# Relational graph network on 100,000 nodes: layer 1 multiplies 112 of 196 blocks, the output stage multiplies 42 parts itself, and implied waits are dropped

## The chip, the cores and the metric

The kernel runs on one core of a Trainium2 chip. The core has TensorE (PE, with weight loads shown as PEld), VectorE (DVE), ScalarE (ACT), GpSimd (POOL) and SyncE (SP), and 16 DMA engines, which the queues of SP (q1), ACT (q10) and POOL (q0, indirect transfers whose descriptors POOL makes itself) share. The metric is the device time of one execution in microseconds. The median of three runs before the change is 3426.85 us (3426.82 to 3428.76); the profiled execution took 3434.24 us, of which the span from first to last instruction is 3432.4 us.

## The reference

```python
h = jnp.maximum(_layernorm(x, axis=-1), 0.0)
x = x + _L0_gnn_ref(h, weight, w_comp, h_bias, src, dst, edge_type_16)
h = jnp.maximum(_layernorm(x, axis=-1), 0.0)
x = x + _L1_gnn_ref(h, enc_w, enc_b, lin_l_w, lin_l_b, lin_r_w, edge_index)   # edge_index = [src, dst]
# _L0: message of an edge = h[src] @ (sum_b w_comp[type, b] * weight[b]); summed by dst; + h_bias
# _L1: h = leaky(x @ enc_w + enc_b)
#      for l in 0, 1:
#          agg = segment_sum(h[src], dst) / max(degree, 1)
#          h = leaky(agg @ lin_l_w[l] + lin_l_b[l] + h @ lin_r_w[l])     (leaky slope 0.1)
```

x is 100,000 x 128 float32 and there are 50,000 edges, sorted by dst. The destinations are drawn as 100000 * u^2, so low rows have most edges.

## The kernel before

The edges are padded to 392 tiles of 128 (56 "half steps" of 7 tiles). Four stages run one after the other, each with its own buffers and semaphores; after a short preparation they are, in the order of the code:

- **Relational stage** (`relational_pass`, 56 steps of 7 tiles). POOL gathers x rows of an edge tile (L368) six steps ahead; DVE takes the norm's statistics (L793 to L808), ACT normalizes (L894), PE transposes and multiplies with the eight bases (L973), ACT and DVE mix the eight products (L912, L826), PE sums runs of equal dst with a 0/1 matrix (`same`, L984), DVE carries a run over the tile's edge (L838), ACT adds the bias (L920) and keeps the rows in one of two buffers of 7 tiles (`rows`, L927), and POOL scatters them to `agg` (L704). In POOL's order one gather of step m and one scatter of step m-6 alternate, and ACT's `keep_rows` of tile (m, j) waits for the scatter of tile (m-2, j) to land. SP meanwhile fills `agg` with the bias (four transfers of 1 MB in each of the first steps, each waiting for the one before the last), stores gathered x rows, and zeroes `means1` and the right half of `pair`. Rows that a scatter must not keep go to spare rows behind row N.
- **Node stage** (`node_pass`): x1 = x + agg, norm, encoder, and layer 0's two products; `pair` holds for each node 128 numbers of h @ lin_r and 128 of the mean's product. POOL again alternates gathers (L1102) and scatters (L1111).
- **Layer 1** (`layer_pass`, the names end in `_l`). POOL gathers 1 KB rows of `pair` for every edge tile (L1722, a ring of three half steps: the gather of step m waits for DVE's addition of step m-3, `s_mixed`). DVE adds the two halves and applies leaky (L1830, L1833); PE sums runs and multiplies with lin_l (L1930, L1938); ACT scales the rows to means (L1885) and stores them by edge, keeping the last eight half steps on chip. In between, a sweep over all nodes makes z1 = leaky(pair sum) @ lin_r + bias: 196 blocks of 512 nodes, seven in each two half steps: SP loads 512 KB of `pair` (L1541), DVE adds and applies leaky (L1550, L1553), PE transposes and multiplies (L1564, L1578, L1582), ACT copies (L1572, L1590) and stores 256 KB to z1 (L1597).
- **Output stage.** POOL puts the means by dst into `means1` (L1727), last half step first; for all but the eight kept ones SP first loads 448 KB back (L1791), and that load waits for the puts of two steps ago. At the same time ACT's queue walks 98 parts of 1024 nodes from the last node down: it loads x1 and z1 three parts ahead (L1684, L1685), waits until enough half steps are put (`wait_final`) and loads the means (L1689), and stores the result of two parts ago (L1696); DVE adds z and mean, applies leaky and adds x1 (L1655, L1658, L1661). Everything on ACT stands in one written order:

```python
for k in range(COUNT + STORED_AFTER):      # STORED_AFTER, LOADED_BEFORE = 2, 3
    if k < COUNT:
        load_means(k)
    if k >= STORED_AFTER:
        store(k - STORED_AFTER)
    if k + LOADED_BEFORE < COUNT:
        load(k + LOADED_BEFORE)
```

## Time and profile before

| | us |
|---|---|
| median of 3 runs | 3426.85 |
| profiled execution | 3434.24 |
| its span | 3432.4 |
| PE / DVE / ACT / POOL busy | 2372.6 / 2910.6 / 1909.4 / 2497.7 |

A share of busy time is an average over the four stages. POOL's instructions here are descriptor generation, each followed by about 0.3 us that the profile calls "issue" and does not count as busy, so POOL can be without a gap and still show 70 to 80%. "DMA" is the busy share of the 16 DMA engines. A row of the timeline gives start, duration, engine, line and names, and in brackets how long the engine stood idle before it and what released it.

### The profile page before, as it was taken

What the parts mean: (1) busy time and instruction counts of PE and PEld (TensorE: products, weight loads), DVE (VectorE), ACT (ScalarE), POOL (GpSimd) and SP (SyncE); (2) the same over time, 40 slices, a digit from 0 to 9 for tenths busy, and PEclk for the clock granted to TensorE, in tenths of its full rate; (3) what the DMA queues carried; (4) which work ended last, traced back from release to release, by engine and by line L of the source; (5) the groups of instructions that cost most, each with busy time, mean ns of one, the idle gap of its engine ahead of it and who ended that gap; (6) DMA issues with size and microseconds to landing.
All of it is one profiled execution on the core that took longest, in us unless ns stands there. A gap on an engine that the chain in (4) does not pass through costs nothing. (4 is left out here: it accounts for less than half of the span.)

```text
span 3432.4 us, 57476 instructions
## 1 busy us (share of the span) xinstructions
PE 2372.6 (69%) x13942; PEld 1758.7 (51%) x13942; DVE 2910.6 (85%) x8326; ACT 1909.4 (56%) x4979; POOL 2497.7 (73%) x2364
## 2 busy tenths in 40 slices
PE   2999999999998688888888888488888860000000
PEld 2555555555554466666666666388778760000000
DVE  4999999899897799999999999699999966555665
ACT  1666666566665688888888888255555540000000
POOL 4777777777776677777777776677777747677675
PEclk9999999999999899999999999799999985555555
DMA  9988888886222899999999997599999979999998
GB/s 242 387 294 263 260 256 257 252 244 178 84 76 66 295 287 282 285 283 282 288 280 289 281 288 219 179 393 401 397 395 395 398 281 412 414 414 414 408 412 313
DMA packets 663813, 1016.37 MB, mean 296 GB/s; under 512 B 73669, under 2 KB 406343, under 8 KB 657058
## 3 DMA queue, kind: packets, MB, share of 16 engines
q1 hardware_dynamic: 487190, 555.28, 49.8%
q10 hardware_dynamic: 94758, 285.20, 21.5%
q0 software_dynamic: 81536, 172.20, 15.1%
q8 instruction: 121, 1.98, 0.2%
q14 instruction: 208, 1.70, 0.1%
HBM read 534.94 MB, written 485.83 MB: 297 GB/s over the span
## 5 line engine op out<-in xcount | busy, mean ns | idle before, releaser
L973 PE MATMUL y_ps_rel<-w_basis,ht_rel 128*128 128x512 f32 x1568 | 745.0, 598 | 0.1
L1722 POOL DMA_INDIRECT gat_l<-base_and_means,src_c x392 | 469.7, 1198 | 123.9 <-issue 118.8
L704 POOL DMA_INDIRECT agg<-rows_rel,put_c x392 | 410.8, 1048 | 135.5 <-issue 98.7
L1270 ACT ACTIVATE h_node<-base_node,shift_node,rstd_node 128x128 f32<-128x128 f32 x1176 | 500.5, 483 | 1.6 <-DVE shift_node L1360 1.6
L368 POOL DMA_INDIRECT gat_rel<-in_x_dram,src_c x392 | 403.7, 1030 | 125.0 <-issue 106.5
L1111 POOL DMA_INDIRECT base_and_means<-rows_node,odd_c x392 | 388.9, 992 | 145.3 <-issue 118.0
L1102 POOL DMA_INDIRECT term_node<-agg,src_c x392 | 395.1, 1008 | 132.9 <-issue 119.7
L1727 POOL DMA_INDIRECT means<-late_l,put_c x336 | 366.9, 1092 | 160.7 <-issue 94.2
L826 DVE SCALAR_TENSOR_TENSOR two_rel<-y_ps_rel,coef,two_rel 128x128 f32<-128x128 f32 x1568 | 437.5, 341 | 3.2 <-DVE two_rel L826 1.8
L973 PEld LDWEIGHTS y_ps_rel<-w_basis,ht_rel 128*128 128x128 f32 x1568 | 269.6, 192 | 192.0 <-issue 131.1
L1655 DVE TENSOR_TENSOR last_z_l<-last_z_l,node_done_l 128x1024 f32<-128x1024 f32 x98 | 120.2, 1226 | 255.9 <-DMA node_done_l<-means 255.8
L984 PEld LDWEIGHTS sum_ps_rel<-same_rel,two_rel 128*128 128x128 f32 x1568 | 237.3, 192 | 188.6 <-issue 111.2
L912 ACT ACTIVATE part_rel<-y_ps_rel,coef 128x128 f32<-128x128 f32 x784 | 243.1, 362 | 139.8 <-PE y_ps_rel L973 139.0
L826 DVE SCALAR_TENSOR_TENSOR two_rel<-y_ps_rel,coef,part_rel 128x128 f32<-128x128 f32 x784 | 237.0, 343 | 77.6 <-ACT part_rel L912 77.3
L1184 PE MATMUL ht_ps_node<-ident,h_node 128*128 128x128 f32 x1176 | 188.8, 283 | 119.6 <-ACT h_node L1270 119.5
L1330 DVE BATCH_NORM_STATS2 st_node<-base_node 128x6 f32<-128x128 f32 x1176 | 256.5, 281 | 10.2
L1184 PEld LDWEIGHTS ht_ps_node<-ident,h_node 128*128 128x128 f32 x1176 | 129.0, 142 | 221.5 <-ACT h_node L1270 221.1
L984 PE MATMUL sum_ps_rel<-same_rel,two_rel 128*128 128x128 f32 x1568 | 238.7, 275 | 0.6 <-DVE sums_rel L838 0.6
L927 ACT ACTIVATE rows_rel<-row_ps_rel 128x128 f32<-128x128 f32 x392 | 108.9, 278 | 203.9 <-PE row_ps_rel L992 130.1
L1582 PEld LDWEIGHTS z_ps_l<-w_r,ht_l 128*128 128x128 f32 x1568 | 209.7, 194 | 7.9
L1217 PEld LDWEIGHTS z_ps_node<-w_r,g_t_node 128*128 128x128 f32 x1568 | 208.2, 193 | 6.6
L1572 ACT ACTIVATE ht_l<-ht_ps_l 128x512 f32<-128x512 f32 x196 | 117.2, 598 | 168.1 <-PE ht_ps_l L1564 124.1
(183 smaller groups left out, 5988.8 us busy)
## 6 DMA issues: line engine op xcount, KB each, us to landing
pairs_l<-base_and_means SPq DMA_DIRECT2D x196, 512.0 KB
base_and_means<-zero_row SPq DMA_DIRECT2D x49, 1024.0 KB
means<-zero_row SPq DMA_DIRECT2D x49, 1024.0 KB
first_node<-in_x_dram SPq DMA_DIRECT2D x196, 256.0 KB
term_node<-agg SPq DMA_DIRECT2D x196, 256.0 KB
x<-base_node SPq DMA_DIRECT2D x196, 256.0 KB
base_and_means<-done_node SPq DMA_DIRECT2D x196, 256.0 KB
z<-node_done_l ACTq DMA_DIRECT2D x196, 256.0 KB
```

What stands on the lines that cost most here:

```text
L368: nc.gpsimd.indirect_dma_start(gat_rel[:, m % X_RING, j, :], None, x, bass.IndirectOffsetOnAxis(ap=src_c[:, m * HALF + j:m * HALF + j + 1] ...
L704: nc.gpsimd.indirect_dma_start(agg, bass.IndirectOffsetOnAxis(ap=put_c[:, t:t + 1], axis=0), rows[:, q, j, :], None).then_inc(s_scattered[ ...
L826: nc.vector.scalar_tensor_tensor(acc[:, a, :], y[:, b * P:(b + 1) * P], c, prior, ALU.mult, ALU.add).then_inc(s_acc, 1)
L973: nc.tensor.matmul(y_ps[(q + j) % 2][:, c * 512:(c + 1) * 512], ht[:, q, j, :], w_basis[:, 4 * c:4 * c + 4, :], start=True, stop=True).the ...
L984: last = nc.tensor.matmul(sum_ps[s][:, 0:P], two[:, j, a, :], same[:, q, j, :], start=(a == 0), stop=(a == 1))
L1102: nc.gpsimd.indirect_dma_start(term[:, q, j * P:(j + 1) * P], None, agg, bass.IndirectOffsetOnAxis(ap=src_c[:, t:t + 1], axis=0)).then_inc ...
L1111: nc.gpsimd.indirect_dma_start(pair.rearrange("n (k f) -> (n k) f", k=2), bass.IndirectOffsetOnAxis(ap=odd_c[:, t:t + 1], axis=0), rows[:, ...
L1184: last = nc.tensor.transpose(ht_ps[n % 2][:, j * P:(j + 1) * P], h[:, n % 2, j * P:(j + 1) * P], ident[:])
L1270: last = nc.scalar.activation(h[:, n % 2, j * P:(j + 1) * P], base[:, n % SLOTS, j * P:(j + 1) * P], ACT.Relu, bias=shift[:, b % 2, c:c + ...
L1330: nc.vector.bn_stats(st6[:, n // 3 % 2, n % 3, j, :], base[:, n % SLOTS, j * P:(j + 1) * P]).then_inc(s_stat, 1)
L1722: nc.gpsimd.indirect_dma_start(gat[:, g, j, :], None, source, bass.IndirectOffsetOnAxis(ap=src_c[:, t:t + 1], axis=0)).then_inc(s_gathered ...
L1727: nc.gpsimd.indirect_dma_start(means1, bass.IndirectOffsetOnAxis(ap=put_c[:, t:t + 1], axis=0), rows_, None, bounds_check=N - 1, oob_is_er ...
```

## The change

Seven things are changed.

1. Layer 1's sweep (`SWEEP = 4` instead of 7) makes four blocks in two half steps, 112 in all. The first 98 are stored to z1 as before. The last 14 (`stays`) are the two halves of each of the last seven parts of nodes; ACT copies their products into the slots of `last_z`, where the output stage finds them, and they aren't stored.
2. The output stage takes the first 7 parts from these slots. For the next 42 parts (`again`) it loads 1 MB of `pair` instead of 512 KB of z1 (`load_pair`), DVE adds and applies leaky (`mix`), PE transposes (`turn_again`), ACT copies (`keep_turned_again`), PE multiplies (`product_again`), and DVE adds the mean to the product in PSUM. The last 49 parts are as before, with z1.
3. In the relational stage the ring of `rows` has three half steps (`KEPT = 3`), with one semaphore for each; ACT waits at j = 0 for all seven scatters of step m-3.
4. The spare rows are doubled (3584), and all of them in `agg` and in both halves of `pair` are zeroed by two transfers at SP's step 2; POOL's first scatter waits for both. Before, 1792 rows of the left half of `pair` were zeroed at the end of the stage.
5. The seven BATCH_NORM_AGGREGATE of a half step and the addition of EPS become five small operations.
6. Waits that another wait implies are left out on DVE, ACT and PE in all stages. POOL's waits stay.
7. In `message` the wait for the low half of the products stands one operation earlier.

```diff
-        SPARE = 2 * HALF * P
+        SPARE = 4 * HALF * P
...
+            KEPT = 3
...
-                rows = buf("rows", [P, 2, HALF, P])
+                rows = buf("rows", [P, KEPT, HALF, P])
...
                         def scatter(m, j):
-                            q, t = m % 2, m * HALF + j
+                            t = m * HALF + j
                             if j == 0:
                                 wait_bias(pool, m)
+                            if m == 0 and j == 0:
+                                pool.wait_ge(s_spare, 2 * DMA)
                             pool.wait_ge(s_rows, tile(m, j))
...
                             spill(m)
+                            if m == 2:
+                                sp.dma_start(agg[N:N + SPARE, :].rearrange("(p j) f -> p j f", p=P),
+                                             zero_row[:].unsqueeze(1).to_broadcast([P, SPARE // P, P])).then_inc(s_spare, DMA)
+                                sp.dma_start(pair[N:N + SPARE, :].rearrange("(p j) (k f) -> p (j k) f", p=P, f=P),
+                                             zero_row[:].unsqueeze(1).to_broadcast([P, SPARE // P * 2, P])).then_inc(s_spare, DMA)
...
-                            for j in range(HALF):
-                                wait_apart(dve, s_dve_passed, (s_stat, tile(m, j)))
-                                nc.vector.bn_aggr(mv[:, q, j, :], st6[:, q, j, :]).then_inc(s_mv, 1)
-                            dve.wait_ge(s_mv, tile(m, HALF - 1))
-                            nc.vector.tensor_scalar(var[:, q, :], mv[:, q, :, 1], EPS, None, ALU.add).then_inc(s_var, 1)
+                            dve.wait_ge(s_stat, tile(m, HALF - 1))
+                            nc.vector.tensor_tensor(apart[:], half[:, :, 1], half[:, :, 4], ALU.subtract).then_inc(s_small, 1)
...
                         def keep_rows(m, q, j):
                             act.wait_ge(s_rowed, tile(m, j))
-                            if at_least(m, 2):
-                                act.wait_ge(s_scattered[q][j], use(m - 2, q))
+                            if m >= KEPT and j == 0:
+                                act.wait_ge(s_scattered[m % KEPT], HALF * DMA * (m // KEPT))
...
-                    return [[(0, 0), (2, 1), (4, 2), (6, 3)], [(1, 4), (3, 5), (5, 6)]][r]
+                    return [[(0, 0), (4, 1)], [(1, 2), (4, 3)]][r]
+                def stays(w, i, c):
+                    return i * w.walk + c >= STORED
...
+                    if stays(w, i, c):
+                        k, a = part_and_half(w, i, c)
+                        result = last_z[:, k, a * BLOCK:(a + 1) * BLOCK]
...
+                AGAIN = COUNT - SLOTS_OUT - STORED // 2
+                def again(k):
+                    return SLOTS_OUT <= k < SLOTS_OUT + AGAIN
...
+                    def mix(k):
+                        dve.wait_ge(s_out[c], k // WALK * DMA)
+                        dve.wait_ge(s_pair[d], (n // len(last_pair) + 1) * DMA)
+                        nc.vector.tensor_tensor(node_.rearrange("p (j f) -> p j f", f=P), last_pair[d][:, :, 0:P],
+                                                last_pair[d][:, :, P:2 * P], ALU.add).then_inc(s_remixed, 1)
...
+                        if again(k):
+                            dve.wait_ge(s_rez, n + 1)
+                            for a in range(2):
+                                nc.vector.tensor_tensor(last_z[:, c, a * BLOCK:(a + 1) * BLOCK], rez_ps[n % 2][a][:],
+                                                        last_m[c][:, a * BLOCK:(a + 1) * BLOCK], ALU.add).then_inc(s_both, 1)
...
+                    for k in range(COUNT):
+                        if again(k + 1):
+                            mix(k + 1)
+                        combine(k)
+                def turn_again(pe, n):
+                    pe.wait_ge(s_releaked, n + 1)
...
+                def product_again(pe, n):
+                    pe.wait_ge(s_reht, n + 1)
...
                         if k >= STORED_AFTER:
                             store(k - STORED_AFTER)
-                        if k + LOADED_BEFORE < COUNT:
+                        if again(k):
+                            keep_turned_again(act, k - SLOTS_OUT)
+                        if again(k + LOADED_BEFORE):
+                            load_pair(k + LOADED_BEFORE)
+                        if SLOTS_OUT <= k + LOADED_BEFORE < COUNT:
                             load(k + LOADED_BEFORE)
```

SP in the relational stage, step 2 (line numbers are those of the changed kernel; L749 loads a step's run starts, L729 stores gathered x rows, L164 fills `agg`, L753 and L755 zero the spare rows):

```order
+L749 DMA run_b_rel<-run_in_tile 128x896 [waits open_made_rel,same_made_rel]
+L729 DMA x_by_edge<-gat_rel 128x896 [waits gathered2_rel]
+L753 DMA agg<-zero_row 3584x1x128
+L755 DMA base_and_means<-zero_row 7168x1x128
+L164 DMA agg<-fill_rows 128x2048 [waits agg_filled1]
```

The two zeroing transfers stand in front of step 2's four fills; before, the first fill followed the x rows directly.

DVE in layer 1, one half step in the middle, before the change:

```order
L1830 TENSOR_TENSOR act_gat_l<-gat_l 128x896
L1833 SCALAR_TENSOR_TENSOR act_gat_l<-act_gat_l 128x896
L1550 TENSOR_TENSOR node_done_l<-pairs_l 128x512
L1553 SCALAR_TENSOR_TENSOR node_done_l<-node_done_l 128x512
L1845 SCALAR_TENSOR_TENSOR sums_l<-open_l,sums_l,sum_ps_l 128x128 x2
L1550 TENSOR_TENSOR node_done_l<-pairs_l 128x512
L1553 SCALAR_TENSOR_TENSOR node_done_l<-node_done_l 128x512
L1845 SCALAR_TENSOR_TENSOR sums_l<-open_l,sums_l,sum_ps_l 128x128 x2
L1814 TENSOR_TENSOR same_l<-run_b_l,run_c 128x896
L1550 TENSOR_TENSOR node_done_l<-pairs_l 128x512
L1553 SCALAR_TENSOR_TENSOR node_done_l<-node_done_l 128x512
```

and the same place in the changed kernel:

```order
L1886 TENSOR_TENSOR act_gat_l<-gat_l 128x896
L1889 SCALAR_TENSOR_TENSOR act_gat_l<-act_gat_l 128x896
L1899 SCALAR_TENSOR_TENSOR sums_l<-open_l,sums_l,sum_ps_l 128x128 x2
L1523 TENSOR_TENSOR node_done_l<-pairs_l 128x512
L1526 SCALAR_TENSOR_TENSOR node_done_l<-node_done_l 128x512
L1899 SCALAR_TENSOR_TENSOR sums_l<-open_l,sums_l,sum_ps_l 128x128 x2
L1874 TENSOR_TENSOR same_l<-run_b_l,run_c 128x896
L1899 SCALAR_TENSOR_TENSOR sums_l<-open_l,sums_l,sum_ps_l 128x128
L1881 TENSOR_SCALAR open_l<-run_b_l 128x896
L1523 TENSOR_TENSOR node_done_l<-pairs_l 128x512
L1526 SCALAR_TENSOR_TENSOR node_done_l<-node_done_l 128x512
```

Of the node sweep's pairs of operations three or four stand in a half step before, two now; the rest of DVE's order is as it was.

ACT in the output stage, one part before the change:

```order
L1689 DMA node_done_l<-means 128x1024
L1696 DMA out_dram<-last_z_l 128x1024
L1684 DMA pairs_l<-x 128x1024
L1685 DMA last_z_l<-z 128x1024
L1668 TENSOR_LOAD need_l
```

and one of the 42 parts in the changed kernel:

```order
L1746 DMA same_l<-means 128x1024
L1753 DMA out_dram<-last_z_l 128x1024
L1712 ACTIVATE ht_l<-ht_ps_l 128x512 x2
L1741 DMA pair_more_l<-base_and_means 128x2048
L1732 DMA pairs_l<-x 128x1024
L1717 TENSOR_LOAD need_l
```

Two ACTIVATEs, which wait for PE's transposes of this part, now stand between the store and the next loads, and a transfer of `pair` of twice the size stands in the place of z1's.

## Rows read from the trace of the kernel before

**Rows 1.** Stages: us, busy (x) of PE, PEld, DVE, ACT, POOL, clock, DMA share, GB/s
```profile
77.00:1122.00 1045.00, 960.00 (x3920) 562.42 (x3920) 936.69 (x3817) 659.70 (x2129) 784.43 (x758) 0.98 0.70 218
1122.00:2181.00 1059.00, 868.35 (x5782) 687.19 (x5782) 993.94 (x3137) 912.79 (x2058) 784.17 (x786) 0.98 0.90 274
2181.00:2774.00 593.00, 490.75 (x3865) 458.57 (x3866) 557.13 (x960) 310.08 (x734) 469.61 (x392) 0.96 1.01 384
...
2836.00:3406.00 570.00, 0.00 (x0) 0.00 (x0) 343.15 (x280) 0.00 (x0) 402.10 (x368) 0.50 1.03 412
```

**Rows 2.** Waits in the relational stage, 230 to 1100 us: total, times, longest
```profile
ACT rows_rel L927 <- DMA agg<-rows_rel,put_c: 73.1, 65, 3.0
...
POOL agg L704 <- ACT rows_rel L927: 25.2, 54, 2.6
```

**Rows 3.** Timeline of POOL: the first scatter
```profile
103.39 1.00 POOL L704 DMA_INDIRECT agg<-rows_rel,put_c  x1 [5.65 <-ACT rows_rel L927]
```

**Rows 4.** DVE's comparison of the run starts, once a step, 130 to 240 us
```profile
L778 DVE TENSOR_TENSOR same_rel<-run_b_rel,run_c x6: 1081/1082/1084, 134.7 to 222.9; 128x896 f32<-128x896 uint8 x6
```

**Rows 5.** Timeline of SP's queue before and in step 2
```profile
79.44 11.19 SPq L164 DMA_DIRECT2D agg<-fill_rows  x4
...
91.17 0.53 SPq L725 DMA_DIRECT2D x_by_edge<-gat_rel  x1
```

**Rows 6.** DMA queue of SP, 400 to 1000 us: packets, MB, share of 16 engines
```profile
q1 hardware_dynamic: 150416, 90.51, 51.9%
```

**Rows 7.** Layer 1: the page's gathers; their durations; DVE's sweep by line, 2240 to 2770
```profile
L1722 POOL DMA_INDIRECT gat_l<-base_and_means,src_c x392 | 469.7, 1198 | 123.9 <-issue 118.8
...
L1722 POOL DMA_INDIRECT gat_l<-base_and_means,src_c x392: 945/1115/9587, 2181.0 to 2773.1; - x196
...
L1553 DVE SCALAR_TENSOR_TENSOR node_done_l<-node_done_l 128x512 f32<-128x512 f32 x173 | 119.7, 692 | 6.0
...
L1550 DVE TENSOR_TENSOR node_done_l<-pairs_l 128x512 f32<-128x512 f32 x173 | 118.2, 683 | 0.1
```

**Rows 8.** Timeline of one long gather and DVE's operation beside it
```profile
2336.79 1.08 DVE L1814 TENSOR_TENSOR same_l<-run_b_l,run_c 128x896 f32<-128x896 uint8 x1
...
2337.01 1.77 POOL L1722 DMA_INDIRECT gat_l<-base_and_means,src_c  x1 [0.30 <-issue]
```

**Rows 9.** Timeline, POOL and DVE: early in layer 1, then its end
```profile
2259.06 1.33 POOL L1722 DMA_INDIRECT gat_l<-base_and_means,src_c  x1 [0.30 <-issue]
...
2267.92 1.08 DVE L1830 TENSOR_TENSOR act_gat_l<-gat_l 128x896 f32<-128x896 f32 x1
...
2773.07 0.94 POOL L1722 DMA_INDIRECT gat_l<-base_and_means,src_c  x1 [0.30 <-issue]
2814.41 1.02 POOL L1727 DMA_INDIRECT means<-kept_rows_l,put_c  x1 [40.39 <-ACT kept_rows_l L1885]
...
2793.00 1.08 DVE L1830 TENSOR_TENSOR act_gat_l<-gat_l 128x896 f32<-128x896 f32 x1
```

**Rows 10.** DMA from 2814 to 3432 us: GB/s in 40 slices, totals, ACT's queue
```profile
GB/s 300 390 416 415 416 416 414 414 416 413 415 415 414 414 414 416 414 414 414 415 415 413 413 414 413 413 413 390 409 406 413 413 413 412 410 406 404 410 169 137
DMA packets 75632, 244.72 MB, mean 396 GB/s; under 512 B 13440, under 2 KB 14281, under 8 KB 75616
...
q10 hardware_dynamic: 56448, 205.55, 82.5%
```

**Rows 11.** Timeline of PE: four transposes twice, then eight matmuls
```profile
2207.19 1.06 PE L1564 MATMUL ht_ps_l<-ident,node_done_l 128*128 128x128 f32 x4
...
2212.54 0.60 PE L1564 MATMUL ht_ps_l<-ident,node_done_l 128*128 128x128 f32 x4
...
2213.20 1.05 PE L1582 MATMUL z_ps_l<-w_r,ht_l 128*128 128x128 f32 x8
```

**Rows 12.** The page's rows of ACT's copy and DVE's addition
```profile
L1655 DVE TENSOR_TENSOR last_z_l<-last_z_l,node_done_l 128x1024 f32<-128x1024 f32 x98 | 120.2, 1226 | 255.9 <-DMA node_done_l<-means 255.8
...
L1572 ACT ACTIVATE ht_l<-ht_ps_l 128x512 f32<-128x512 f32 x196 | 117.2, 598 | 168.1 <-PE ht_ps_l L1564 124.1
```

More of the change, by code:

```diff
@@ L712, in _ @@
                                     scatter(m - lag, j)
-                        for q in range(2):
-                            for j in range(HALF):
-                                pool.wait_ge(s_scattered[q][j], DMA * HALVES // 2)
+                        for k in range(KEPT):
+                            pool.wait_ge(s_scattered[k], HALF * DMA * len(range(k, HALVES, KEPT)))
                     @block.sync
@@ L1670, in wait_base @@
                 def wait_base(act):
-                    act.wait_ge(s_need, 1)
-                    for c in range(sweep.walk):
-                        act.wait_ge(sweep.s_stored[c], DMA * walks)
+                    for c in range(SWEEP):
+                        act.wait_ge(sweep.s_stored[c], DMA * len(range(c, STORED, SWEEP)))
                 def write_out(act):
@@ L1698, in write_out @@
                     wait_base(act)
-                    for k in range(LOADED_BEFORE):
+                    act.wait_ge(s_need, 1)
+                    for k in range(SLOTS_OUT):
                         load(k)
@@ L1956, in _ @@
                             ago(HALVES, 0, 0, j, 3, to_rows)
+                        for n in range(AGAIN):
+                            turn_again(pe, n)
+                            product_again(pe, n)
             clear(held)
```

256 lines of the change are left out of this document (129 added, 127 removed).

## Prediction

> **What bounds the kernel now.** I read the stages first [rows 1]. In the output stage the 16 DMA engines are full (share 1.03, 412 GB/s) and PE and ACT are empty; in layer 1 they are full too (1.01, 384 GB/s), but something else is also full there. So I read POOL. Its share of busy time looks harmless, because about 0.30 us after each transfer aren't counted [rows 8, 9]. With them a gather of layer 1 takes 1.198 us + 0.30 [rows 7], and 392 of them fill 588 of the stage's 593 us; only 5.0 us go to waits for DVE. In the relational stage POOL's mean is 784.43 / 758 = 1.035 us [rows 1], and a step has 7 gathers and 7 scatters: 14 x 1.335 = 18.7 us. DVE, left alone, makes a step in (222.9 - 134.7) / 5 = 17.64 us [rows 4]. POOL falls behind by a microsecond a step until ACT finds no free buffer: 65 stalls, 73.1 us [rows 2]. The reader should see that this isn't time to be won: in 870 us POOL waited 25.2 us for rows [rows 2]. POOL sets the pace of this stage. The node stage is alike: 784.17 us in 786 transfers, with 0.30 each 1020 of 1059 us [rows 1], and nothing is changed on POOL there.
>
> **The change, part by part**, against the profiled execution's 3434.24 us.
>
> *Relational stage, third buffer and dropped waits: 0.* They free ACT and DVE, which POOL already outruns. The wait at j = 0 for all of step m-3 lets POOL be later by about one tile's time at the stage's end, 1 us. The five small operations of DVE take the place of eight; DVE has a microsecond a step to spare, so they count nothing. If POOL weren't the pace, DVE's 17.64 us would come true instead of 18.7: 50 steps x 1.06 = -53 us; that is the lower bound of this item, the upper is +5 (small operations with two SBUF inputs in POOL's way).
>
> *Zeroing of the spare rows: +14 us.* Two transfers of 3584 and 7168 rows of 512 B go in front of step 2's fills, and the first scatter, which stood at 103.39 us [rows 3], now waits for them. Behind it in POOL's order stand all later gathers and scatters. SP reaches the place at 91.17 + 0.53 us [rows 5]; the four fills before it took 11.19 us, 2.8 each, and two of them are under way, with the 448 KB spill behind: start about 98 us. Price: a packet of this queue, while it mostly writes 512 B zeros, took 0.519 x 16 x 600 us / 150,416 = 33 ns of one engine [rows 6]; 10,752 packets over 16 engines are 22 us. They land at about 120 us, 16.6 after 103.39, of which POOL gets back the wait of 1 to 2 us that followed. Since POOL never idles afterwards, it goes through to the end: +14. Bounds: 0 (if the engines take the zeros first) and +20. The .9 MB zeroing that leaves the end of the stage was hidden there: 0.
>
> *Node stage: 0*, -5 to +5.
>
> *Layer 1, the gathers: -22 us.* The shortest gather is 945 ns, the mean 1198 [rows 7]. What is the rest? The gather at 2337.01 began 0.22 us into DVE's comparison of 1.08 us and took 1.77 us, that is, the comparison's remaining 0.86 us (less a little) longer [rows 8]. So a gather that meets a long DVE operation with two SBUF inputs waits for its end. Random arrivals meet an operation of length t in proportion to t and lose t/2: the sum of t²/2 over a half step is 3.5 x (0.683² + 0.692²)/2 = 1.65 for the sweep [rows 7], and 3 x 1.08²/2 = 1.75 for the comparison and the two additions over the gathered rows [rows 8]. The sweep's 1.65 becomes 2 x 0.473 = 0.95: together 3.40 to 2.70, x 0.79. In a step shortened from 10.6 to 10.2 us they come denser: the excess of 0.253 us becomes 0.21. A half step is then 7 x (0.945 + 0.21 + 0.30) = 10.2 us, and 56 of them 571 instead of 593. Bounds: no excess left, 56 x 8.7 = 488 (-105); the excess unchanged, 0. DVE, at 557 of 593 us [rows 1], loses 84 x 1.4 = 118 us of work; DMA falls from 228 MB (593 us x 384) to 158: neither is near. That is where most of the expected gain stays out: the sweep was cut by 43%, but POOL gathers as before.
>
> [...]
>
> *Layer 1, its end: -17 us.* The last gather starts at 2773.07, DVE adds its half step at 2793.00, and the first put is at 2814.41 [rows 9]. Early in the stage that first distance was 2267.92 - 2260.4 = 7.5 us instead of 19: DVE had fallen behind to the depth of the ring. With 118 us less work it doesn't: -12. The last 21.4 us hold DVE's and ACT's last blocks and stores; half of the blocks and all stores of the end go: -5. Bounds -5 and -27.
>
> *Output stage: +34 us.* Before, 244.72 MB [rows 10] at 412 GB/s [rows 1] are 594 us; the stage has 618 (2814.4 to 3432.4), the other 24 being the start (300 and 390 GB/s in the first slices of 15.45 us: 5 us) and the end (169 and 137: 19 us [rows 10]), where the last part waits for the last put. Now 49 parts load no z1 (49 x 0.524 = -25.69 MB; 98 before) and 42 load 1.049 MB of `pair` (+44.04): 263.07 MB, 638.5 us. The start stays 5. The puts, 604 us long before, end ahead of the transfers, so the end is only the last part's additions and store, 8 us: 651.5, +33.5. The added work must hide: DVE per part 2 x 1.23 for `mix` and about 4.0 to combine [rows 12], 6.5 us; one part is 2.62 MB at 412 less the 69 GB/s of the puts and loads back ((244.72 - 205.55) MB / 570 us [rows 10]), 7.6 us. It hides, with 1 us of room. Bounds: +25 (start gap gone too) and +55 (below).
>
> Sum: 14 - 22 - 17 + 34 = +9. Profiled 3443 us; as this execution was 7.4 above the median, the median is forecast at 3426.85 + 9 = **3436 us**.
>
> **Rivals.**
>
> *Slow clock in the output stage (slower).* The chain of one part is PE transposes, ACT's two copies (1.15 us [rows 12]), PE products, and PE takes the next part's transposes only after that. At the upper clock it is short: 8 transposes 1.05, 16 products and two bias products 2.4 [rows 11], with two hand-overs of 0.25: 5.1 us. At the lower level (1.2 GHz, as at 2207.19, where four transposes took 1.06 instead of 0.60 us [rows 11]) it is 1.9 + 1.15 + 4.6 + 0.5 = 8.15 us a part. It decides from 7.6 us on: 42 x 0.55 = +23, so 3459. For it: PE stands still 40 us before and has half a part's time idle in each part. Against it: between 2207.19 and 2212.54 the same kind of work brought the upper level back [rows 11]. No row shows work with pauses like these.
>
> *The relational stage gains (faster).* If ACT's 73.1 us of stalls, not POOL, cost the time, a third buffer gives up to -53; I take half, -26 instead of 0: 3410. Against it stand POOL's waits of 25.2 us in 870.
>
> *Gathers near their floor (faster).* If DVE's and POOL's steps lock so that they seldom meet, half of the excess goes: 56 x 9.6 = 538, -55 instead of -22: 3403. The steps here are regular, so phase matters; nothing says which.
>
> *The zeroing is hidden (same).* If it lands before about 105 us: +9 - 14 = -5, 3422.
>
> *The change doesn't do what it says:* product and store of fewer blocks, but no time; that is nearly the forecast's own statement, since -39 and +34 cancel.
>
> **How the numbers follow.** Forecast 45%, slow clock 17%, relational gain 9%, gathers near the floor 9%, zeroing hidden 12%, others 8%. A measurement of this kernel can tell 0.2%, 7 us, from no change: slower is above 3434, faster below 3420. The forecast's own range, from the bounds, is 3418 to 3455; of its 45%, 27 are slower, 15 the same and 3 faster. Slower: 27 + 16 (slow clock) + 3 (hidden) + 4 (others) = 50%. Same: 15 + 1 + 7 (hidden) + 3 = 26%. Faster: 3 + 8 + 8 (the two faster rivals) + 2 + 3 = 24%. The range that leaves out 2 in 10 goes from 3403 to 3463.
>
> **What would show it.** Right: the first scatter near 120 us, POOL without waits after it and the first node gather (1122 before) near 1136; gathers of layer 1 with a mean of 1.15 us and the first put 41 - 17 = 24 us after the last gather; the output stage at 412 GB/s from the first parts to the end, 263 MB, the last put some 45 us before the last store. Wrong: a relational step below 18 us in the middle; a gather mean below 1.08; an output stage in which the DMA share falls below 1 in the 42 parts (the slow clock, or the written order on ACT).

## The result, and the profile after

The changed kernel takes 3400.98 us (median of 4 runs, 3400.85 to 3402.68), the kernel before on the same chip 3427.81 us (4 runs): a ratio of 0.9921, with a 95% interval of 0.9904 to 0.9939. It is 27 us faster. Ratios leave out executions that took over 1.5% longer than the fastest of the same kernel. The forecast was 3436 us, 9 us slower, with a range from 3403: both the sign and the range were wrong.

The profiled execution has a span of 3399.1 us (3432.4 before). Its stages, in the columns of [rows 1]; the fourth line is the output stage, the fifth the 42 parts that are made again:

```profile
77.00:1147.00 1070.00, 969.20 (x3920) 568.78 (x3920) 930.39 (x3649) 664.73 (x2129) 786.38 (x757) 0.97 0.70 217
1147.00:2203.00 1056.00, 865.72 (x5782) 685.23 (x5782) 992.26 (x3137) 911.91 (x2058) 782.41 (x786) 0.98 0.90 275
2203.00:2716.00 513.00, 380.46 (x2870) 352.43 (x2871) 464.29 (x812) 243.85 (x582) 393.60 (x392) 0.95 0.94 320
2741.00:3399.00 658.00, 204.05 (x1092) 176.63 (x1092) 463.46 (x420) 45.58 (x84) 421.80 (x392) 0.62 1.00 400
2783.00:3106.00 323.00, 204.05 (x1092) 176.63 (x1092) 261.19 (x255) 45.58 (x84) 219.58 (x201) 0.75 1.02 414
```

The reader should see two things. Layer 1's gathers take 513 us instead of 593 with POOL's 392 transfers at 393.60 us instead of 469.61 [rows 1]; the forecast had 571. And in the parts made again the DMA engines are full (1.02) though PE's clock is at 0.75 in the mean.

| stretch | before | after | difference | forecast |
|---|---|---|---|---|
| up to the first gather of layer 1 | 2181.0 | 2202.9 | +21.9 | +14 |
| gathers of layer 1 | 592.1 | 511.9 | -80.2 | -22 |
| last gather to first put | 41.3 | 26.8 | -14.5 | -17 |
| output stage | 618.0 | 657.4 | +39.4 | +34 |
| sum | | | -33 | +9 |

(us of the profiled executions; the medians of the runs differ by 27.)

**Start.** The timelines of POOL and of SP's queue (start, duration, idle time before it and what ended it), which answer to [rows 3, 5]:

```profile
128.01 0.99 POOL L709 DMA_INDIRECT agg<-rows_rel,put_c  x1 [31.05 <-DMA base_and_means<-zero_row]
...
92.24 11.20 SPq L164 DMA_DIRECT2D agg<-fill_rows  x4
103.55 0.39 SPq L749 DMA_DIRECT2D run_b_rel<-run_in_tile  x1
104.39 0.54 SPq L729 DMA_DIRECT2D x_by_edge<-gat_rel  x1
104.98 1.06 SPq L753 DMA_DIRECT2D agg<-zero_row  x1
106.09 7.51 SPq L755 DMA_DIRECT2D base_and_means<-zero_row  x1
```

The first scatter stands at 128.01, not near 120. SP reaches step 2 only at 103.55: the row at 91.17 of [rows 5], which I took for step 2's, was step 1's, and another four fills of 11.20 us lie between. The price was right: issued at 104.98, released at 128.01 are 23 us, against the 22 that I worked out.

**Relational stage.** The waits from 230 to 1100 us, which answer to [rows 2]:

```profile
ACT rows_rel L925 <- DMA agg<-rows_rel,put_c: 39.0, 23, 2.1
POOL agg L709 <- ACT rows_rel L925: 17.1, 56, 0.3
```

ACT's stalls fell from 73.1 to 39.0 us, and the stage took as long as before: first to last scatter 1005.2 us (128.0 to 1133.2), before 1004.4.

**Layer 1.** The page's row of the gathers and the spread of their durations, which answer to [rows 7]; below them POOL and then DVE in the middle of the stage:

```profile
L1784 POOL DMA_INDIRECT gat_l<-base_and_means,src_c x392 | 393.7, 1004 | 119.7 <-issue 119.7
...
L1784 POOL DMA_INDIRECT gat_l<-base_and_means,src_c x392: 942/946/10308, 2202.9 to 2714.8; - x196
...
2500.28 0.94 POOL L1784 DMA_INDIRECT gat_l<-base_and_means,src_c  x1 [0.30 <-issue]
2501.53 0.94 POOL L1784 DMA_INDIRECT gat_l<-base_and_means,src_c  x1 [0.30 <-issue]
...
2499.26 1.08 DVE L1886 TENSOR_TENSOR act_gat_l<-gat_l 128x896 f32<-128x896 f32 x1
2500.38 1.09 DVE L1889 SCALAR_TENSOR_TENSOR act_gat_l<-act_gat_l 128x896 f32<-128x896 f32 x1
```

The median gather is now at the floor of 0.94 us. Look at the place of DVE's two long operations, both with two SBUF inputs: the first ends at 2500.34, 0.06 us after a gather's start, the second starts at 2500.38, 0.10 us after it. One gather starts every 0.94 + 0.30 = 1.24 us, two of DVE's operations of 1.08 us are 1.12 apart, and neither costs POOL anything.

**End of layer 1.** POOL's last gather and first put, which answer to [rows 9]:

```profile
2714.85 0.95 POOL L1784 DMA_INDIRECT gat_l<-base_and_means,src_c  x1 [0.30 <-issue]
2741.67 1.02 POOL L1789 DMA_INDIRECT means<-kept_rows_l,put_c  x1 [25.88 <-ACT kept_rows_l L1939]
```

**Output stage.** DMA from 2742 to 3399 us: GB/s in 40 slices of 16.4 us, and the totals, which answer to [rows 10]:

```profile
GB/s 313 289 410 418 416 417 416 416 418 417 416 415 416 415 417 417 417 414 415 417 415 398 400 414 413 414 414 413 412 413 413 413 404 413 412 403 389 407 405 168
DMA packets 74614, 263.14 MB, mean 401 GB/s; under 512 B 13328, under 2 KB 14169, under 8 KB 69209
```

263.14 MB were moved, where 263.07 were worked out.

### The profile page after: what moved, and what is told of

The parts are those of the page before. It is cut to its first block and busy times, and to the rows that moved or that the text cites. A ratio compares the mean times of both kernels' runs of the same rounds, so it can differ in the third digit from the quotient of the medians.

```text
span 3399.1 us, 49875 instructions
## 1 busy us (share of the span) xinstructions
PE 2460.3 (72%) x13942; PEld 1821.4 (54%) x13942; DVE 2901.5 (85%) x8116; ACT 1885.1 (55%) x4895; POOL 2417.1 (71%) x2364
## 3 DMA queue, kind: packets, MB, share of 16 engines
q14 instruction: 165, 1.35, 0.1%
## 5 line engine op out<-in xcount | busy, mean ns | idle before, releaser
L972 PE MATMUL y_ps_rel<-w_basis,ht_rel 128*128 128x512 f32 x1568 | 754.9, 605 | 3.7 <-DVE two_rel L831 3.7
L1784 POOL DMA_INDIRECT gat_l<-base_and_means,src_c x392 | 393.7, 1004 | 119.7 <-issue 119.7
L1984 PE MATMUL sum_ps_l<-same_l,act_gat_l 128*128 128x128 f32 x784 | 169.5, 299 | 153.9 <-DVE sums_l L1899 112.8
L1712 ACT ACTIVATE ht_l<-ht_ps_l 128x512 f32<-128x512 f32 x84 | 45.6, 595 | 312.9 <-PE ht_ps_l L1692 312.9
L1984 PEld LDWEIGHTS sum_ps_l<-same_l,act_gat_l 128*128 128x128 f32 x784 | 119.8, 193 | 176.0 <-DVE act_gat_l L1889 149.8
```

The source lines that it names most:

```text
L972: nc.tensor.matmul(y_ps[(q + j) % 2][:, c * 512:(c + 1) * 512], ht[:, q, j, :], w_basis[:, 4 * c:4 * c + 4, :], start=True, stop=True).the ...
L1784: nc.gpsimd.indirect_dma_start(gat[:, g, j, :], None, source, bass.IndirectOffsetOnAxis(ap=src_c[:, t:t + 1], axis=0)).then_inc(s_gathered ...
L1984: nc.tensor.matmul(sum_ps[(q + j) % 2][:, 0:P], act_gat[:, q, j, :], same[:, q, j, :], start=True, stop=True).then_inc(s_summed, 1)
```

## The experiments

Theory after the result: a gather of layer 1 lasts 0.945 us, and longer only where it starts inside a DVE operation that holds it up; the excess (what a gather takes over 0.945 us) fell further than I had thought. Rivals: the 16 DMA engines, full before (1.01), lengthened the gathers; the third buffer won time. Medians are compared with the kernel before on the same chip (ratio, 95% interval). A trace is of one execution, and not always of a typical one; where it took much longer or shorter than the median, the text says so.

**The zeroing, and the relational stage.** In the first kernel the spare rows of `agg` are zeroed ahead of step 0's fills, and those of `pair` at the stage's end; the first scatter waits for the former alone:

```diff
-                            if m == 2:
+                            if m == 0:
                                 sp.dma_start(agg[N:N + SPARE, :] ...
-                                sp.dma_start(pair[N:N + SPARE, :] ...
...
+                        sp.dma_start(pair[N:N + SPARE, :] ...
```

> The changed kernel, with the spare rows of agg zeroed ahead of the fills of step 0 (not of step 2), the first scatter waiting for those alone, and the spare rows of base_and_means zeroed at the end of the relational stage. Theory (the late first scatter goes through to the end, since POOL sets the pace of the stage): first scatter back at 103 to 106 us (128.0 in the changed kernel, 103.4 before), last one at 1108 to 1111, and the whole 22 to 25 us faster than the changed kernel: 3376 to 3379. Rival (POOL catches up in the stage, so that the delay cost little): last scatter near 1125 to 1133, gain below 8 us.

Measured: 3388.52 us, ratio 0.9885 (0.987 to 0.990): 12.5 us less than the changed kernel, half of what I expected. First scatter at 103.1, last at 1116.2. But the profiled execution took 3401.71 us, 13 above the median and as long as the changed kernel, so its rows don't show what a typical one won.

The second is the changed kernel with the whole old `relational_pass` and 3584 spare rows.

> The changed kernel with the relational stage of the kernel before (two row buffers, all of its waits, bn_aggr, 3584 spare rows and their zeroing at the end); layer 1 and the output stage as changed. Theory (the third buffer and the dropped waits are worth nothing, POOL sets the pace; only the zeroing cost): first gather of the node stage at 1122, as before, and 22 to 26 us faster than the changed kernel: 3375 to 3379, the same as with the zeroing moved. Rival (the third buffer gains, hidden by the zeroing): slower than the kernel with the zeroing moved by what the buffer is worth, by the 73 - 39 us of ACT's stalls up to 34 us.

Measured: 3375.61 us (5 runs), ratio 0.9847 (0.9834 to 0.986), 25 us below the changed kernel, as expected (profiled: 3384.96). It is **faster than both kernels**. First scatter at 104.3, last at 1108.9. From first to last scatter it takes 1004.6 us, the changed kernel 1005.2: the third buffer and the dropped waits gained nothing. With the zeroing hidden the new stage took 1013.1 in the one execution that was profiled, the long one; the medians point the same way, since that kernel is 12.9 us slower than the one with the old stage. POOL's transfers sum to 820 us there and to 811 in the old stage, and POOL waits 45.7 us for rows instead of 36.6. Where the transfers met DVE's comparison, the excess over 945 ns was 33 against 27 us; to the five small operations I put about 2. That is most of the 9 us of transfers, not a cause that was shown. The run meant for it changed only the mean and variance back:

> The kernel with the zeroing moved, with the mean and variance of the kernel before (bn_aggr on one SBUF input, seven times a step) in place of the five small operations on DVE, four of them with two SBUF inputs. With the zeroing moved the relational stage ended at 1116.2 us, with the old stage at 1108.9, and its gathers and scatters took 820 us against 811. Theory (the small operations hold POOL up, as those of layer 1 do): last scatter at 1107 to 1111 us, POOL's transfers 811 to 815 us, the whole 5 to 10 us faster than with the zeroing moved alone. Rival (the third buffer or the dropped waits or the place of the zeroing cost it): last scatter 1114 to 1118, no change of the whole.

It fell on a chip on which both kernels took longer (4162.27 us, the kernel before 4177.82; ratio 0.994, 0.9896 to 0.9985), and can't be set beside the others. Why the new stage costs time stays open.

**More and fewer blocks.** `SWEEP` 5 and 3, other lists of places (with 3, `store` also skips a block that does not exist, and one more buffer holds means):

```diff
-                SWEEP = 4
+                SWEEP = 5          # the other kernel: 3
-                    return [[(0, 0), (4, 1)], [(1, 2), (4, 3)]][r]
+                    return [[(0, 0), (2, 1), (4, 2)], [(1, 3), (4, 4)]][r]   # 3: [[(0, 0), (4, 1)], [(2, 2)]]
```

> The changed kernel with 5 blocks of the sweep per two half steps (places (0, 2, 4) and (1, 4)) instead of 4: 126 blocks stored, 28 parts made again. Theory (gathers are lengthened by DVE's operations with two SBUF inputs, which meet them more often again): gather mean 1.04 to 1.10 us, layer 1's gathers 530 to 550 us (513 with 4, 593 with 7), output stage 13 us shorter than 657, whole 3408 to 3425. Rival (the gathers' time goes by what the 16 DMA engines have to move): the bytes of layer 1 rise from 164 to about 186 MB, 362 GB/s in 513 us, below the 384 to 416 that the engines did: gathers stay at 513 to 518 us, whole 3388 to 3395.

> The changed kernel with 3 blocks per two half steps (places (0, 4) and (2)): 70 blocks stored, 56 parts made again. Theory: the excess over 945 ns, already 59 ns in the mean, shrinks only a little (gather mean 0.97 to 0.99, gathers 500 to 508 us), the output stage grows by 14 x 0.94 = 13 us, the end of layer 1 is some 3 us shorter: 3394 to 3405, no gain. Rival (excess in proportion to the sweep, 80 us for three blocks): 27 us off the gathers, 3382 to 3390.

Measured: with 5 blocks 3404.72 us (0.9934, 0.9919 to 0.9949), gather mean 1.043, gathers 527 us, as the theory had it, the gathers and the whole each 3 us under its range. With 3 blocks 3453.41 us (1.0078, 1.0063 to 1.0094): **less work on DVE, less on the DMA, and the gathers take 551 us instead of 512**, mean 1.104. With 3 blocks the theory and its rival both missed. How much DVE does was not the point.

**The same work at other places.**

```diff
-                    return [[(0, 0), (4, 1)], [(1, 2), (4, 3)]][r]
+                    return [[(1, 0), (5, 1)], [(2, 2), (6, 3)]][r]
```

> Again the changed kernel with the four blocks at the places (1, 5) and (2, 6), on a chip that runs at the usual speed. After the runs so far the theory is another: whether an operation of DVE stands where a gather starts is a matter of where the operations are, not of how little DVE does (with 3 blocks the mean was 1.104, with 4 at (0, 4), (1, 4) it was 1.004). Expected: gather mean 1.08 to 1.17 us as on the slow chip (1.157), gathers of layer 1 545 to 575 us, whole 30 to 60 us slower than the changed kernel. Rival (DVE that keeps up is enough, the slow chip spoilt the first try): mean 0.98 to 1.05, gathers 505 to 530 us.

Measured: 3475.64 us, ratio 1.0145 (1.012 to 1.0169), 75 us above the changed kernel, where I expected 30 to 60. Here is the same stretch of that kernel: the page's row, POOL, DVE.

```profile
L1784 POOL DMA_INDIRECT gat_l<-base_and_means,src_c x392 | 468.3, 1195 | 119.7 <-issue 119.7
...
2500.38 1.35 POOL L1784 DMA_INDIRECT gat_l<-base_and_means,src_c  x1 [0.30 <-issue]
2502.03 1.43 POOL L1784 DMA_INDIRECT gat_l<-base_and_means,src_c  x1 [0.30 <-issue]
...
2499.82 1.09 DVE L1886 TENSOR_TENSOR act_gat_l<-gat_l 128x896 f32<-128x896 f32 x1 [2.90 <-DMA gat_l<-base_and_means,src_c]
2501.96 0.68 DVE L1523 TENSOR_TENSOR node_done_l<-pairs_l 128x512 f32<-128x512 f32 x1
```

Every operation is the one of the changed kernel; the mean is back at 1.195 us (1.198 before) and the gathers at 586 us. The first gather starts with 0.53 us of the addition left and takes 1.35 us, 0.40 over 0.945; the second with 0.61 us left, 0.48 over. So what is left of the operation, less 0.13 us, is added. The whole gain of layer 1 hangs on four numbers in a list.

**DVE's load and the DMA's load, one at a time.** One kernel gives DVE 84 pairs of operations more in layer 1 (on a scratch buffer, at places of their own), the other SP 112 loads of 512 KB more that nobody reads:

```diff
+  nc.vector.tensor_tensor(pair_more[:, 4:6, :] ..., pair_more[:, 0:4, 0:P], pair_more[:, 0:4, P:2 * P], ALU.add)
+  nc.vector.scalar_tensor_tensor(pair_more[:, 4:6, :], pair_more[:, 4:6, :], SLOPE, pair_more[:, 4:6, :], ALU.mult, ALU.max)
```

```diff
+  for a in range(2):
+      sp.dma_start(pair_more[:, 4 * a:4 * a + 4, :], pair[m * BLOCK:m * BLOCK + BLOCK, :] ...)
```

> Again the changed kernel with DVE's old work in layer 1 (84 further pairs of operations on a scratch buffer), on a chip at the usual speed. Theory (gathers are lengthened by DVE's operations with two SBUF inputs and by nothing else): gather mean 1.15 to 1.22 us, gathers 570 to 600 us with the DMA engines at 280 to 290 GB/s. Rival (the DMA load made them long): mean 0.99 to 1.03.

> Again the changed kernel with 58.7 MB of further loads in layer 1, on a chip at the usual speed. Theory: gathers that start in no two-input operation of DVE take 0.945 us as ever; 223 MB at 412 GB/s are 541 us, so that layer 1's gathers take 535 to 560 us, the addition of waiting for data (over 20 us) and not of longer gathers; mean 0.97 to 1.08 (the places shift). Rival (full DMA engines lengthen the gather itself): also gathers that meet no operation of DVE are longer than 1.0 us.

Measured: 3492.29 us (1.0193, 1.0169 to 1.0218) and 3467.91 us (1.0122, 1.0097 to 1.0147). Their layer 1, in the columns of [rows 1]:

```profile
2204.00:2793.00 589.00, 419.20 (x2834) 388.78 (x2834) 560.34 (x961) 239.38 (x577) 458.27 (x392) 0.88 0.86 277
...
2204.00:2776.00 572.00, 391.98 (x2834) 362.64 (x2834) 463.38 (x802) 242.04 (x577) 434.31 (x392) 0.93 1.01 384
```

With DVE's old work and 277 GB/s the gathers take as long as before (mean 1.170): less traffic alone does not make them short. With full engines they take 572 us, longer than the 541 that the bytes need and longer than I expected, and the mean is 1.108. But in that kernel DVE waits 65.2 us for `run_b` loads, which now queue behind the further ones, and so stands at other places. Of 349 gathers, 153 meet a long operation and carry 51.4 of the 51.8 us of excess; the other 196 took 0.947 us in the mean, with the engines full. The DMA doesn't lengthen a gather; it moves DVE.

**The rule over all kernels.** For each gather (the first 29 and last 14 left out, 349 stay) I took what was left, at its start, of a DVE operation with two SBUF inputs; where this was over 0.15 us, it less 0.13 us is what the rule adds:

| kernel | gathers us | mean us | that meet one | excess over 0.945, sum us | by the rule | DVE waits for rows | POOL waits for DVE |
|---|---|---|---|---|---|---|---|
| before | 592 | 1.198 | 236 | 82.2 | 77.0 | 1.4 | 5.0 |
| changed | 512 | 1.004 | 78 | 11.8 | 8.8 | 2.9 | 0 |
| old relational stage | 512 | 1.004 | 73 | 12.2 | 8.6 | 0 | 0.3 |
| 5 blocks | 527 | 1.043 | 102 | 25.1 | 22.0 | 3.1 | 0 |
| 3 blocks | 551 | 1.104 | 131 | 48.0 | 49.4 | 42.8 | 0 |
| other places | 586 | 1.195 | 178 | 80.8 | 80.1 | 53.4 | 0 |
| DVE more | 588 | 1.170 | 207 | 72.1 | 64.8 | 0 | 17.0 |
| DMA more | 571 | 1.108 | 153 | 51.8 | 49.4 | 3.4 | 28.9 |
| zeroing moved | 518 | 1.017 | 86 | 16.5 | 12.7 | 0.8 | 2.2 |
| before, other places | 589 | 1.188 | 203 | 79.2 | 73.4 | 0.6 | 6.6 |
| pieces, marks on ACT | 521 | 1.028 | 105 | 20.4 | 39.6 | 11.4 | 0 |
| pieces | 548 | 1.050 | 89 | 29.0 | 25.7 | 0 | 22.1 |

(The last three kernels are described below.) The rule gives the excess of every kernel but one to within 8 us, from 9 to 80. For "pieces, marks on ACT" it gives twice the measured excess. Two gathers of that kernel, each with DVE's operation beside it, show why:

```profile
2309.40 0.95 POOL L1784 DMA_INDIRECT gat_l<-base_and_means,src_c  x1 [0.30 <-issue]
2309.36 0.77 DVE L1526 SCALAR_TENSOR_TENSOR node_done_l<-node_done_l 128x512 f32<-128x512 f32 x1
...
2344.93 1.46 POOL L1784 DMA_INDIRECT gat_l<-base_and_means,src_c  x1 [0.30 <-issue]
2344.88 0.69 DVE L1526 SCALAR_TENSOR_TENSOR node_done_l<-node_done_l 128x512 f32<-128x512 f32 x1
```

The first operation began 0.04 us before the gather: the gather lost nothing, and the operation took 0.77 us itself. The second began 0.05 us before, took its usual 0.69 us, and the gather lost 0.52. In this kernel 26 gathers began less than 0.045 us behind such an operation; the rule adds 20.2 us for them, and they carry 0.01. Without them it gives 19.4 for 20.4 us. In the 20 traces together 61 gathers that began up to 0.043 us behind an operation were free, and of 104 held ones that began up to 0.12 us behind it all but one stood at 0.045 or more. So the remainder counts only where the operation came first by some 0.045 us. I read this off the traces; no run was made to test it.

The last two columns (from the views of the waits) show what goes with few meetings: in four quick kernels (changed, old relational stage, zeroing moved, 5 blocks) DVE hardly waits for gathered rows, nor POOL for DVE's addition. Where DVE does wait for rows, the landing of a transfer starts its additions, at any place between two gathers; where POOL waits for the ring, DVE works without a pause and leaves no room. The kernel before has neither and was slow, and the one with the marks on ACT was quick with 11.4 us of waits, so this goes with it but is not a proof.

**Were the places enough, without the cut?** The kernel before, seven blocks at (0, 1, 4, 5) and (1, 4, 5):

> Again the kernel before with its seven blocks at the places (0, 1, 4, 5) and (1, 4, 5), on a chip at the usual speed. Theory (DVE's 9.95 us of work in a half step of 10.6 leave it no room to stand clear of the gathers): gather mean 1.12 to 1.25 us, gathers 570 to 615 us, whole 3405 to 3450. Rival (places alone do it): mean 1.05 or less, gathers at 557 to 565 us.

Measured: 3427.89 us, ratio 0.9997 (0.9987 to 1.0006), gathers 589 us, mean 1.188. With DVE busy for 556 of 589 us these places gave nothing. Together with the same work at other places (586 us): the cut at other places gained nothing, and these places without the cut gained nothing; the cut with its own places had the gain. Of places with seven blocks only this one other list has been tried.

**Other forms of operations**, on top of the old relational stage. The comparison as seven `tensor_scalar` (one SBUF tensor each), and in the first of the two kernels the marks of open runs made by ACT:

```diff
-  nc.vector.tensor_tensor(same[:, q, :, :], columns(q), run_c[...].to_broadcast([P, HALF, P]), ALU.is_equal)
+  for j in range(HALF):
+      last = nc.vector.tensor_scalar(same[:, q, j, :], columns(q)[:, j, :], run_c[:, bass.ds(m * HALF + j, 1)], None, ALU.is_equal)
-  nc.vector.tensor_scalar(open_[:, q, :, :], columns(q), 0.0, None, ALU.is_equal)          # first kernel only
+  nc.scalar.activation(open_[:, q, :, :], run_b[:, q, :] ..., ACT.Relu, bias=ones[:, 0:1], scale=-1.0)
```

> The changed kernel with the relational stage of before, and in layer 1 the comparison as seven tensor_scalar operations (one SBUF input each) in place of one tensor_tensor with two, and the marks of open runs made on ACT (Relu of 1 - run). Theory (only operations with two SBUF inputs hold a gather up): the comparison's share of the excess (7.5 us of 12 with the old relational stage) goes, gather mean 0.965 to 0.99, gathers 498 to 508 us against 511.7, whole 3360 to 3372 (3375.6 with the relational stage alone). Rival (any DVE operation of that place holds it up, or the seven operations shift others in the way): mean 1.00 or more, whole 3373 to 3400.

> Again the old relational stage and the comparison of layer 1 in seven single-input pieces, the marks of open runs on DVE, on a chip at the usual speed. Theory (DVE a little behind the gathered rows starts its operations right after a gather's start and holds up none): lag over 8 us, gather mean 0.965 to 1.00, gathers 498 to 510 us, and with 0.6 us more a half step for DVE faster than with the marks on ACT (3386): 3362 to 3374. Rival (less work on DVE is better in any case): mean 1.03 or more, no faster than 3386.

Measured: 3386.46 us (0.989, 0.9869 to 0.9912) and 3410.78 us (0.9948, 0.9934 to 0.9962), gathers 521 and 548 us. The profiled executions took 3378.5 and 3423.72 us, 8 below and 13 above the medians. Neither kernel reaches the ratio of the old relational stage alone (0.9847): both of my expectations missed, and the rivals were right, each in its part. In the second, DVE fell behind until POOL waited for it (22.1 us). While the lag from a half step's last gather to its addition grew from 8 to 18 us (half steps 5 to 13), the gathers' excess was 31 ns in the mean; from half step 16 on, at the depth of the ring, 100 ns.

An operation with one SBUF input can hold a gather up too, but here it is the marks of open runs and not the pieces. POOL and DVE of the second kernel, then of the first, where ACT makes the marks:

```profile
2238.46 1.21 POOL L1784 DMA_INDIRECT gat_l<-base_and_means,src_c  x1 [0.30 <-issue]
...
2237.70 1.06 DVE L1875 TENSOR_SCALAR same_l<-run_b_l,run_c 128x128 f32<-128x128 uint8 x5
2238.68 0.34 DVE L1900 SCALAR_TENSOR_TENSOR sums_l<-open_l,sums_l,sum_ps_l 128x128 f32<-128x128 f32 x1
2238.93 0.62 DVE L1882 TENSOR_SCALAR open_l<-run_b_l 128x896 f32<-128x896 uint8 x1
...
2308.15 0.95 POOL L1784 DMA_INDIRECT gat_l<-base_and_means,src_c  x1 [0.30 <-issue]
...
2307.40 1.07 DVE L1875 TENSOR_SCALAR same_l<-run_b_l,run_c 128x128 f32<-128x128 uint8 x5
2308.38 0.34 DVE L1895 SCALAR_TENSOR_TENSOR sums_l<-open_l,sums_l,sum_ps_l 128x128 f32<-128x128 f32 x1
2308.63 0.69 DVE L1523 TENSOR_TENSOR node_done_l<-pairs_l 128x512 f32<-128x512 f32 x1
```

In both the last piece ends some 0.3 us after the gather's start. The first gather took 0.27 us over 0.945 and ends at 2239.67, 0.12 us after the marks (2239.55); the second lost nothing. Of the second kernel's 49 gathers that start in a piece, 26 have no marks starting 0.4 to 0.65 us later and carry 0.07 us of excess together; 18 of the other 23 end 0.12 us after the marks and carry 5.8 us. In the changed kernel 25 gathers end so, with 2.4 us beyond the rule, most of the 3.0 that it lacks there; with the marks on ACT none does. So my rule is too narrow. The Trainium skill (SBUF — State Buffer, "SBUF: two separate sides") says that a DVE operation in a mode that uses two ports shuts GpSimd out of the pair of ports that they share, and that whichever of the two starts first has the pair for its whole instruction. The marks fit the first half: 896 numbers a partition took 0.62 us, where the comparison takes 1.08, and the gathers end right behind them. The second half does not fit, since these gathers had started 0.47 us and more before the marks. No run tells which mode the marks were in, or what lets them in.

**Runs on other chips.** Eight runs fell on two chips where the kernel before took 4182 and 4178 us. The untouched node stage was longer there: in the kernel with the old blocks at other places PE's granted clock was 0.86 in the mean from 1450 to 2700 us, against 1.00 in the kernel before from 1200 to 2100 us on a usual chip, while DVE's addition over the gathered rows took 1.085 us on both. Against the kernel before of the same chip:

> The changed kernel, with 84 further pairs of DVE operations in layer 1 (an addition and a leaky step over 128x512, both inputs in SBUF, on a scratch buffer, without DMA, PE or ACT work), so that DVE does what it did in the kernel before while the DMA does what it does in the changed one. Theory (DVE's operations lengthen the gathers): gather mean back to 1.15 to 1.22 us, gathers of layer 1 570 to 600 us, lag from gather to addition 19 us or so again, whole 60 to 85 us slower than the changed kernel. Rival (the DMA load made them long): gather mean 0.99 to 1.02, gathers 513 to 530 us.

> The changed kernel, with 112 further loads of 512 KB in layer 1 that nobody uses (58.7 MB, two per half step, on SP), so that the DMA moves 223 MB there, as in the kernel before (228), while DVE does what it does in the changed one. Theory (DVE's operations lengthen the gathers; the DMA is only a floor): 223 MB at 412 GB/s are 541 us: gathers of layer 1 take 535 to 555 us, POOL waits for DVE, whose data come late, and the median of a gather stays at 0.95 to 0.99 us. Rival (full DMA engines lengthen the gather itself): gather mean and median back to 1.1 to 1.2 us, gathers 580 to 600 us.

> As the kernel with 112 further loads, but with 56 of them (29.4 MB, one per half step): 194 MB in layer 1. Theory: 194 MB at 412 GB/s are 470 us, below the 513 that POOL needs, so nothing moves: gather mean 0.99 to 1.02 us, gathers 511 to 520 us. Rival (DMA load sets the gathers' time): half of the way back, mean 1.08 to 1.12, gathers 545 to 560 us.

> The changed kernel with the four blocks of the sweep at other places among the seven tiles of a half step ((1, 5) and (2, 6) instead of (0, 4) and (1, 4)); all work the same. Theory (DVE keeps up and its operations start on what the gathers and PE deliver, so that they stand in a fixed place between two gathers and seldom meet a start): the mean depends little on the places, 0.98 to 1.05 us, gathers 505 to 530 us. Rival (it was luck of these four places): a mean near 1.155, what random meetings give, gathers 560 to 575 us.

> The kernel before, all work the same, its seven blocks at the places (0, 1, 4, 5) and (1, 4, 5) instead of (0, 2, 4, 6) and (1, 3, 5). Theory (the excess is a matter of places, but DVE's 9.95 us of work in a half step are a floor under it): gather mean between 1.12 and 1.25 us, gathers of layer 1 570 to 615 us, at best 557; whole 3405 to 3450. Rival (places alone do it, the cut of the work was not needed): gathers at 557 to 565 us, mean at 1.05 or less.

> The changed kernel with the old relational stage and the comparison of layer 1 as seven single-input operations, the marks of open runs left on DVE (0.6 us a half step more for DVE than when they were on ACT). Theory (where DVE waits for the gathered rows, at a lag of 5 to 7 us, its operations start at any place between two gathers; where it is a little behind, they start right after a gather's start and hold up none): DVE is behind again, lag over 8 us, gather mean 0.965 to 1.00, gathers 498 to 510 us, faster than with the marks on ACT although DVE does more: whole 3362 to 3374. Rival (less work on DVE is better in any case): mean at 1.03 or more, no faster than 3386.

> The old relational stage, comparison in seven pieces, marks of open runs on ACT, and 5 blocks of the sweep per two half steps (0, 2, 4) and (1, 4). With 5 blocks in the changed kernel 17.8 of 25 us of excess were the comparison's. Theory: DVE is behind the gathered rows again (lag over 8 us), mean 0.97 to 1.01, gathers 500 to 520 us, output stage 641: 3355 to 3370, the fastest so far. Rival (the places shift to bad ones): mean 1.05 to 1.10, 3375 to 3400.

Measured, in this order: 4077.3 (0.9741), 4168.95 (no ratio), 4178.94 (0.9943), 4079.59 (0.9747), 4143.45 (0.9944), 4252.84 (1.0159), 4225.16 us (1.0101), with gather means of 1.201, 1.052, 1.083, 1.157, 1.202, 1.082 and 1.116. POOL waited up to 213.5 us for DVE in layer 1 there (31.7 us in the first), so none of the times decides between the theories, and the kernels with 56 further loads, with the old mean and variance, and with 5 blocks and other forms have no run at the usual speed. The rule holds within these runs too: with the 84 further pairs the excess was 84.2 us and the rule gives 80.7, with the 112 loads 30.4 and 29.4.

## Why the prediction was wrong

- **What bounds the kernel** was right: POOL's transfers with 0.30 us each set the pace of layer 1 and of the relational stage.
- **Relational stage, third buffer: 0.** Right (1005.2 us against 1004.6 with the old stage). That the new stage costs more when the zeroing is hidden (12.9 us between the medians, 8 in the stage of the executions profiled) was not foreseen (my bound was +5), and its cause is open.
- **Zeroing: +14, measured +25** at the first and at the last scatter, above my bound of +20. The duration was right; the place of step 2 in SP's queue was read one step too early. The node stage (0, -5 to +5) gave 3.4 back, so that +21.9 was left at layer 1's first gather.
- **Gathers of layer 1: -22, measured -80.** This is the step that failed. The mechanism (a gather waits for the rest of a DVE operation) was right and gives nearly all of the excess, once the marks and the order of the starts are added to it. Wrong was "random arrivals": DVE and POOL are locked to each other, and where the operations stand repeats, in the changed kernel, every two half steps. At other places the same operations cost 586 us, nearer to the 571 forecast. That the four places chosen were good ones was luck: nothing in the prediction chose them. The rival "gathers near their floor" named the mechanism, with 9% and 538 us; 512 were measured. My bounds, -105 to 0, held the value, but the range of the whole was drawn from the rivals and not from these bounds: 3403 as its lower end had no ground in them.
- **End of layer 1: -17, measured -14.5.** Right in size: -8 of it from the last gather to its addition (19.9 to 11.9 us), where -12 were forecast, and -6.5 behind it, for -5.
- **Output stage: +34, measured +39.4.** Bytes right to 0.1 MB. The start lost 9 us (313 and 289 GB/s in the first two slices) and not 5, the end 10 and not 8; between them the rate was that of the forecast. The rival "slow clock" did not decide: PE's clock fell to 0.75 in the parts made again, and the DMA stayed full.
- Sum: the gathers' term was wrong by 58 us; the other way went the start (zeroing and node stage) by 8, the output stage by 5 and the end of layer 1 by 2.5.

## What to carry to other kernels

Where GpSimd issues indirect transfers one after another beside a busy VectorE, find for each transfer what is left, at its start, of a VectorE operation with two SBUF inputs that began before it: that remainder, less 0.13 us, was nearly all of the excess here, and it is a matter of places, which a regular schedule repeats in every step. Don't average over such phases; treat them as two cases with a price each, and try a few orders of the same work, since here four numbers in a list were worth 75 us. Before a buffer or a wait is taken for the reason of a gain, put the old stage back under the new rest: here that alone made the fastest of the kernels run.

## What was not expected of the hardware

- A DVE operation with two SBUF inputs that starts 0.01 to 0.10 us after a gather's start costs it nothing (94 such gathers in the changed kernel, excess 1 ns in the mean), and one that ends 0.06 us after it doesn't either; one with 0.53 us left costs 0.40. Begun up to 0.043 us before the gather it was free too (61 gathers).
- DVE's marks, with one SBUF input, held gathers up though they started after them (by 0.47 us in the row shown): the gather ended 0.12 us after the marks, 18 times with the pieces and 25 times in the changed kernel.
- Two chips took 4178 and 4182 us for a kernel that takes 3428 on the others. Which kernel was the faster was another there in some cases: the one with other places (1.0145 of the kernel before) was at 0.9747.
